# A routed MoE block: the down projection in five products of 128 + 48 features, and router logits with both weight halves side by side

## The chip, the cores and the metric

The kernel runs on one core of one Trainium2 chip. The metric is the device time of one execution in microseconds (us). A core has TensorE (PE; its weight loads are listed as PEld), VectorE (DVE), ScalarE (ACT), GpSimd (POOL) and the queue of SyncE (SP), which issues most of the transfers.

## The reference

A transformer block with adaptive layer norm over 8 batches of 256 tokens of width 256. Attention first, and then a mixture of experts: a router picks two of 8 experts for each token, and a shared expert runs for all. Cut to what matters here:

```python
logits = h @ gate_weight.T                      # 256 -> 8 experts
scores = softmax(logits); topk_w, topk_i = group_limited_topk(scores)   # 2 of 8
g = einsum('th,nfh->ntf', h, gate_w)            # expert: 256 -> 176
u = einsum('th,nfh->ntf', h, up_w)
e = einsum('ntf,nhf->nth', silu(g) * u, down_w) # 176 -> 256
routed = einsum('nth,tn->th', e, wmat)          # weighted sum over the two experts
shared = silu(h @ sh_gate_w.T) * (h @ sh_up_w.T) @ sh_down_w.T
```

## The kernel before

Everything is written by hand: each engine has its own list of steps, in a fixed order, and semaphores tie them together. Products run on operands split in a high part (fp32r) and a low part, the rest. `mm3` (lines 339 to 343) makes one product of two split operands with three instructions: low x high (L341), high x low (L342), high x high (L343).

The first 200 us hold attention for the 8 batches, layer norm, the shared expert (`pe_up`, `pe_down`) and the router, interleaved on all engines. The router of a batch: `pe_logits` multiplies the router weights `wrt` (256 x 8, two blocks of 128 rows, so 2 x `mm3` = six products of 256 columns) with the transposed tokens `h2T` into 8 rows of a bank; `act_lg` copies them to `lg`; for each pair of batches `pe_logits_t` (L551) transposes four pieces of 8 x 128 with the identity, and VectorE selects the experts from the result (`dve_select`). GpSimd scatters each token's row, with its metadata, to the region of its experts in memory (`pool_scatter`).

In the same time the experts' weights are brought in: `sp_weights` (L1254, L1256) loads the gate and up weights and the down weights of one expert into one of two staging buffers `wstage`, `act_weights` (L1271, L1272) copies the high part into `experts_w`, and `split_weights` (L1277, L1278) subtracts it for the low part, on GpSimd or VectorE in turn. The 176 features of the down weights lie as two halves of `FH` = 88 rows side by side.

From some 205 us on the routed loop runs over NT = 39 tiles of 128 rows, as a hardware loop of four tiles a round with a few tiles unrolled at both ends (`steps`). For a tile t, by engine:

- SP loads the 128 rows (`sp_tile`, L1290), after the activation of the tile four earlier.
- TensorE transposes the rows (`pe_tile_in`, L1302, two); `pe_tile_up` makes six products of 352 columns (gate and up); `pe_tile_act` transposes the activation (L1324, two, 88 features each); `pe_tile_down` makes six products of 256 columns, 88 rows each. In one round its order is up(t+1), transposes of the activation(t), transposes of the rows(t+3), down(t-1).
- ScalarE: `act_tile_silu` (L1341) for t+1, the high half of the transposed activation `act_tile_act` (L1345) for t, of the rows `act_tile_in` (L1337) for t+3, and the output copy `act_tile_out` (L1350) for t-1.
- VectorE: metadata (`dve_tile_meta`, L1363 `second`, L1365 `wt`, L1367 `dest`) and activation (`dve_tile_act`, L1374) for t+1, then the low half `dve_tile_lo` (L1380) for t and `dve_tile_in` (L1354) for t+3. The metadata waits until the scatter of the tile four earlier has landed, as `dest` has four buffers.
- GpSimd scatters the 128 output rows (`pool_tile`, L1385) after the copy of L1350.

After the last tile SP reads the routed rows back, and VectorE and GpSimd add them to the residual (`final`).

Of the kernel before, what the change touches and what calls it, by code (L numbers as in the profile page):

```python
# [8 lines left out]
ALU = mybir.AluOpType  # L9
# [7 lines left out]
ds = bass.ds  # L17
# [11 lines left out]
def adaln_block(nc, x_in, w_qkv, b_cols, w_proj, b_proj, gate_col, cam_w0, cam_w1,  # L29
# [12 lines left out]
    FH = F // 2  # L42
    FT = [(f, min(P, FS - f)) for f in range(0, FS, P)]
    UNR = 3
    assert D == KD * P == 256 and S == TT * P == 256 and NT % UNR == 0 and F <= 256

    with ExitStack() as ctx:
# [20 lines left out]
        s_const_dve = sem("const_dve")  # L68
        s_whi_later = sem("whi_later")
        s_wlo_later = sem("wlo_later")  # L70
        s_a_hi = sem("a_hi")
# [166 lines left out]
        wrt = hilo("wrt", [P, KD, NE])  # L238
# [23 lines left out]
        lg = [sb(f"lg{u}", [NE, S]) for u in range(2)]  # L262
# [278 lines left out]
        def act_lg(act, b):  # L541
# [3 lines left out]
            act.activation(lg[b % 2][:], post_bank(b)[0:NE, 0:S], ACT.Copy).then_inc(s_lg_copied, 1)  # L545
# [172 lines left out]
        if True:  # L718
# [80 lines left out]

            def pool_setup(pool):  # L800
# [120 lines left out]
            def dve_guard(dve):  # L921
# [12 lines left out]
                dve.tensor_tensor(mrow[:, 1, :], mrow[:, 0, :], bprow[:], ALU.mult).then_inc(s_mrow_ready, 1)  # L934

# [293 lines left out]
            avT = [tuple(h[0:FH, 1, q * S:(q + 1) * S].rearrange("p (k n) -> p k n", k=2) for h in h2T) for q in range(2)]  # L1229

            sg = [wstage[q][:, 0:F] for q in range(2)]
            av = [wstage[q][:, F:2 * F] for q in range(2)]
            yo = [wstage[q % 2][:, 2 * F + q // 2 * D:2 * F + (q // 2 + 1) * D] for q in range(4)]
# [6 lines left out]
            def expert(e, part, at, n):  # L1240
                base = (0, W1, 2 * W1, 2 * W1 + W2)[part]
                return experts_w[0:(P if part < 2 else FH), ds(e * WE + (base + at), n)]
# [7 lines left out]
            def sp_weights(sp, e, r):  # L1250

                if e >= 2:
# [920 lines left out]
```

## Time and profile before

| | us |
|---|---|
| median of three runs | 331.73 |
| lowest, highest | 330.33, 333.68 |
| profiled execution | 331.29 |
| its span, from the first to the last instruction | 329.5 |
| TensorE busy | 266.7 (81%) |
| VectorE busy | 219.1 (66%) |
| ScalarE busy | 157.2 (48%) |
| GpSimd busy | 147.4 (45%) |

Times in the rows count from the span's start. TensorE's instructions overlap: a product is listed with its whole way through the array (0.28 us for 256 columns), and the next one starts long before its end. What a product costs in a dense stretch is therefore the step from start to start, not the duration. Idle time of an engine is put down to what ended it.

### The profile page before, as it was taken

What the parts mean: (1) busy time and instruction counts of PE and PEld (TensorE: products, weight loads), DVE (VectorE), ACT (ScalarE), POOL (GpSimd) and SP (SyncE); (2) the same over time, 40 slices, a digit from 0 to 9 for tenths busy, and PEclk for the clock granted to TensorE, in tenths of its full rate; (3) what the DMA queues carried; (4) which work ended last, traced back from release to release, by engine and by line L of the source; (5) the groups of instructions that cost most, each with busy time, mean ns of one, the idle gap of its engine ahead of it and who ended that gap; (6) DMA issues with size and microseconds to landing.
All of it is one profiled execution on the core that took longest, in us unless ns stands there. A gap on an engine that the chain in (4) does not pass through costs nothing.

```text
span 329.5 us, 6560 instructions
## 1 busy us (share of the span) xinstructions
PE 266.7 (81%) x1796; PEld 245.4 (75%) x1797; DVE 219.1 (66%) x672; ACT 157.2 (48%) x421; POOL 147.4 (45%) x159
## 2 busy tenths in 40 slices
PE   2799999789999999889968934499999999994000
PEld 2797699579999999779967924499999999993000
DVE  2757664895288735979899984166667766661396
ACT  1457767568466884444423310346555565552000
POOL 2111219612251689568548674014444444444370
PEclk9999999979999999979999996589999999998555
DMA  6990035442012124034201134523434344320894
GB/s 228 315 284 15 1 117 147 130 131 66 32 35 82 50 93 135 0 111 118 50 23 68 58 131 146 178 62 108 125 111 126 115 121 117 111 83 1 289 316 159
DMA packets 30191, 37.78 MB, mean 115 GB/s; under 512 B 4452, under 2 KB 24783, under 8 KB 30168
## 3 DMA queue, kind: packets, MB, share of 16 engines
q1 hardware_dynamic: 25896, 29.02, 29.6%
q0 software_dynamic: 3408, 8.46, 7.3%
q8 instruction: 11, 0.18, 0.2%
q10 hardware_dynamic: 864, 0.02, 0.1%
q14 instruction: 12, 0.10, 0.1%
HBM read 25.83 MB, written 12.57 MB: 117 GB/s over the span
## 4 chain that ended last, share of the span: by engine, by line
PE 61%; DVE 20%; issue 6%; DMA 6%; ACT 3%; SPq 1%; ACTq 1%; POOL 1%; POOLq 0%; DVEq 0%
PE bank L341 14%; PE bank L342 13%; PE bank L343 13%; PE bank L1089 4%; DMA routed_out<-wstage,dest 3%; PE bank L1324 2%; PE bank L1302 2%; PE bank L1072 2%; PE bank L1044 2%; DVE experts_w L1420 2%; DMA experts_w<-routed_out 2%; DVE h2all L499 2%; DVE experts_w L1418 2%; PE bank L1081 1%; DVE aact L440 1%
## 5 line engine op out<-in xcount | busy, mean ns | idle before, releaser
L1385 POOL DMA_INDIRECT routed_out<-wstage,dest x39 | 38.4, 984 | 58.6 <-ACT wstage L1350 40.6
L341 PE MATMUL bank<-experts_w,h2T_lo 128*128 (+1 forms) x156 | 52.8, 338 | 0.6 <-DVE h2T_lo L1354 0.6
L342 PE MATMUL bank<-experts_w,h2T_hi 128*128 (+1 forms) x156 | 48.1, 308 | 0.0
L343 PE MATMUL bank<-experts_w,h2T_hi 128*128 (+1 forms) x156 | 47.9, 307 | 0.0
L662 POOL DMA_INDIRECT routed_in<-h2all,slot_u x32 | 32.6, 1019 | 16.3 <-DVE slot_u L648 8.7
L341 PEld LDWEIGHTS bank<-experts_w,h2T_lo 128*128 128x128 f32 (+1 forms) x156 | 30.2, 194 | 2.4 <-issue 1.7
L342 PEld LDWEIGHTS bank<-experts_w,h2T_hi 128*128 128x128 f32 (+1 forms) x156 | 30.4, 195 | 0.0
L341 PE MATMUL bank<-h2T_hi,wsgu_lo 128*128 128x256 f32 (+1 forms) x96 | 28.3, 294 | 2.3 <-DVE og L458 2.3
L343 PEld LDWEIGHTS bank<-experts_w,h2T_hi 128*128 128x128 f32 (+1 forms) x156 | 30.0, 192 | 0.0
L343 PE MATMUL bank<-h2T_hi,wsgu_hi 128*128 128x256 f32 (+1 forms) x96 | 27.0, 281 | 0.0
L342 PE MATMUL bank<-h2T_lo,wsgu_hi 128*128 128x256 f32 (+1 forms) x96 | 27.0, 281 | 0.0
L1341 ACT ACTIVATE wstage<-bank 128x176 f32<-128x176 f32 x39 | 12.4, 317 | 25.7 <-PE bank L343 25.7
L448 POOL TENSOR_TENSOR aT_lo<-aact,aT_hi 128x256 fp32r<-128x256 f32 (+1 forms) x15 | 11.9, 803 | 24.4 <-ACT aT_hi L431 24.3
L1337 ACT ACTIVATE h2T_hi<-bank 128x256 fp32r<-128x256 f32 x39 | 14.5, 373 | 17.3 <-PE bank L1302 17.1
L341 PE MATMUL bank<-hT_hi,wqk_lo 128*128 128x256 f32 x64 | 20.7, 323 | 1.5 <-DVE hT_lo L1174 1.5
L341 PE MATMUL bank<-wsd_hi,aT_lo 128*128 128x256 f32 (+1 forms) x48 | 14.9, 309 | 7.7 <-DVE aT_lo L448 7.7
L1363 DVE TENSOR_TENSOR second<-exchange,eid_off 128x1 f32<-128x1 f32 x39 | 6.2, 158 | 22.0 <-DMA routed_out<-wstage,dest 22.0
L1350 ACT ACTIVATE wstage<-bank 128x256 f32<-128x256 f32 x39 | 15.0, 384 | 12.2 <-PE bank L343 12.2
L1302 PE MATMUL bank<-ident,exchange 128*128 128x128 f32 x78 | 15.7, 288 | 5.6 <-DMA exchange<-routed_in 5.6
L1354 DVE TENSOR_TENSOR h2T_lo<-bank,h2T_hi 128x256 fp32r<-128x256 f32 x39 | 16.0, 411 | 6.0 <-ACT h2T_hi L1337 6.0
L341 PEld LDWEIGHTS bank<-h2T_hi,wsgu_lo 128*128 128x128 f32 (+1 forms) x96 | 17.4, 181 | 2.6 <-DVE og L458 2.5
L342 PE MATMUL bank<-hT_lo,wqk_hi 128*128 128x256 f32 x64 | 19.3, 301 | 0.0
(225 smaller groups left out, 829.0 us busy)
## 6 DMA issues: line engine op xcount, KB each, us to landing
exchange<-routed_in SPq DMA_DIRECT2D x39, 130.0 KB, 2.1
experts_w<-routed_out SPq DMA_DIRECT2D x16, 256.0 KB, 5.7
wstage<-gu_t SPq DMA_DIRECT2D x8, 352.0 KB
res<-x SPq DMA_DIRECT2D x4, 512.0 KB, 9.2
mx<-modrow SPq DMA_DIRECT2D x8, 256.0 KB, 3.1
mh<-modrow SPq DMA_DIRECT2D x8, 256.0 KB, 3.6
out<-res SPq DMA_DIRECT2D x8, 256.0 KB, 2.3
wmod_s<-w_mod SPq DMA_DIRECT2D x3, 512.0 KB, 10.1
```

Of the source, the lines that this page charges most:

```text
L341: pe.matmul(out_ap, l[1], r[0], start=start, stop=False)
L342: pe.matmul(out_ap, l[0], r[1], start=False, stop=False)
L343: return pe.matmul(out_ap, l[0], r[0], start=False, stop=stop)
L448: eng.tensor_tensor(aT[q % 2][1][0:m, j, :], aact[n % 2][0:m, :], aT[q % 2][0][0:m, j, :].bitcast(F32), ALU.subtract).then_inc(s_a_lo_dve ...
L662: pool.indirect_dma_start(out=routed_in, out_offset=bass.IndirectOffsetOnAxis(slot_u[:, i, j:j + 1], 0), in_=h2all[:, j % (2 * NB), :], in ...
L1089: last = pe.matmul(TR[u][:, t * D:(t + 1) * D], PT[u][:, k, t * P:(t + 1) * P], VV[u][:, k, P:P + D], start=(k == 0), stop=(k == TT - 1))
L1302: last = pe.transpose(XTb[r % 2][:, d * P:(d + 1) * P], xt_in[r][:, d * P:(d + 1) * P], ident[:])
L1337: act.activation(eT[r][0], bank2(XTb[r % 2], P), ACT.Copy).then_inc(s_ex_hi, 1)
L1341: act.activation(sg[r % 2], EGU[r % 2][:, 0:F], ACT.Silu).then_inc(s_esilu, 1)
L1350: act.activation(yo[r], EDN[r % 2][:, 0:D], ACT.Copy).then_inc(s_ey_ready, 1)
L1354: dve.tensor_tensor(eT[r][1], bank2(XTb[r % 2], P), eT[r][0].bitcast(F32), ALU.subtract).then_inc(s_ex_lo, 1)
L1385: pool.indirect_dma_start(out=routed_out, out_offset=bass.IndirectOffsetOnAxis(dest[r][:, 0:1], 0), in_=yo[r], in_offset=None, bounds_chec ...
```

## The change

The activation of a tile is laid out in two blocks of 128 columns for two of 88: features 0 to 127, and then features 128 to 175 twice, at columns 0 to 47 and 64 to 111 of the second block, with zeros between. After the transposes (now 128 columns each) ScalarE writes the high half of all; VectorE writes the low half of the first block, and in the second block it writes the low half over the rows 64 to 111 of the *high* operand. So one operand of 112 rows holds the high and the low half of the 48 features. The down weights are staged the same way, the last 48 rows twice. The down projection then is `mm3` over 128 rows, one product of 112 rows (high and low of the 48 features times the high weights) and one of 48 rows (high times the low weights).

The router's weights stand side by side, 8 high and 8 low columns, so that a product with the high and one with the low half of the tokens give 16 rows; the two sets of 8 are added where they were transposed, by a product with `fold2` (two identities on top of each other, an fp32 product and no longer a transpose). It includes the product of both low parts, which was left out.

Moved or added around it: the down weights of an expert come in three transfers for one; GpSimd sets the rows between to zero before the first one (`pool_stage_rows`), for which SP waits; VectorE makes `fold2` first of all, and the zeros of the activation buffers before the first tile (`dve_tile_gaps`); the activation of a tile has a second multiplication of 48 columns, and the low half is made in two parts.

```diff
-    FH = F // 2
+    FB = F - P
+    HALF = P // 2
...
-        wrt = hilo("wrt", [P, KD, NE])
+        wrt_both = sb("wrt_both", [P, KD, 2 * NE], F32R)
+        wrt = (wrt_both[:, :, 0:NE], wrt_both[:, :, NE:2 * NE])
+        fold2 = sb("fold2", [2 * NE, NE])
...
             for k in range(KD):
-                last = mm3(pe, post_bank(b)[0:NE, 0:S], parts(wrt, slice(None), k),
-                           parts(h2T, slice(None), k, ring4(b)), k == 0, k == KD - 1)
+                for i in range(2):
+                    last = pe.matmul(post_bank(b)[0:2 * NE, 0:S], wrt_both[:, k, :], h2T[i][:, k, ring4(b)],
+                                     start=(k + i == 0), stop=(k + i == KD))
...
-                last = pe.transpose(LOG[:, j * NE:(j + 1) * NE], lg[j // TT][:, j % TT * P:(j % TT + 1) * P], ident[0:NE, 0:NE])
+                last = pe.matmul(LOG[:, j * NE:(j + 1) * NE], lg[j // TT][:, j % TT * P:(j % TT + 1) * P], fold2[:], start=True, stop=True)
...
+            def pool_stage_rows(pool):
+                for r in range(2):
+                    for rows in (slice(P // 4, HALF), slice(HALF + P // 4, P)):
+                        pool.memset(wstage[r][rows, W1 + D:], 0.0).then_inc(s_stage_zero, 1)
+                pool.wait_ge(s_stage_zero, 4)
...
+            def dve_fold2(dve):
+                dve.wait_ge(s_ident_ready, 1)
+                dve.tensor_tensor(fold2[:], ident[0:2 * NE, 0:NE], ident[0:2 * NE, NE:2 * NE], ALU.add)
...
-                sp.dma_start(wstage[r][0:FH, W1:].rearrange("p (j n) -> p j n", j=2),
-                             down_t[ds(e, 1)].rearrange("o (j p) n -> p (o j) n", p=FH)).then_inc((s_est0_in, s_est1_in)[r], 16)
+                down = down_t[ds(e, 1)].rearrange("o f n -> f (o n)")
+                for to, of in ((wstage[r][:, W1:W1 + D], down[0:P]), (wstage[r][0:FB, W1 + D:], down[P:F]),
+                               (wstage[r][HALF:HALF + FB, W1 + D:], down[P:F])):
+                    sp.dma_start(to, of).then_inc((s_est0_in, s_est1_in)[r], 16)
...
-                act.wait_ge((s_est0_in, s_est1_in)[r], 16 * (e - r) + 32)
+                act.wait_ge((s_est0_in, s_est1_in)[r], 64 * (e // 2 + 1))
...
-                    last = pe.transpose(ATb[r % 2][0:FH, j * P:(j + 1) * P], av[r % 2][:, j * FH:(j + 1) * FH], ident[:])
+                    last = pe.transpose(ATb[r % 2][:, j * P:(j + 1) * P], av[r % 2][:, j * P:(j + 1) * P], ident[:])
...
-                for j in range(2):
-                    last = mm3(pe, EDN[r % 2][:, 0:D], parts(avT[r % 2], slice(None), j),
-                               (expert(e, 2, j * D, D), expert(e, 3, j * D, D)), j == 0, j == 1)
-                last.then_inc(s_edn_done, 1)
+                to, (hi, lo) = EDN[r % 2][:, 0:D], avT[r % 2]
+                mm3(pe, to, (hi[:, 0], lo[:, 0]), (expert(e, 2, 0, D), expert(e, 3, 0, D)), True, False)
+                pe.matmul(to, hi[0:HALF + FB, 1], expert(e, 2, D, D, HALF + FB), start=False, stop=False)
+                pe.matmul(to, hi[0:FB, 1], expert(e, 3, D, D, FB), start=False, stop=True).then_inc(s_edn_done, 1)
...
-                dve.scalar_tensor_tensor(av[q], sg[q], wt[q][:, 0:1], EGU[q][:, F:2 * F],
+                dve.scalar_tensor_tensor(av[q][:, 0:F], sg[q], wt[q][:, 0:1], EGU[q][:, F:2 * F], ALU.mult, ALU.mult)
+                dve.scalar_tensor_tensor(av[q][:, P + HALF:F + HALF], sg[q][:, P:F], wt[q][:, 0:1], EGU[q][:, F + P:2 * F],
                                          ALU.mult, ALU.mult).then_inc(s_ea_ready, 1)
...
-                dve.tensor_tensor(avT[q][1], bank2(ATb[q], P)[0:FH], avT[q][0].bitcast(F32), ALU.subtract).then_inc(s_ea_lo, 1)
+                hi, lo = avT[q]
+                second_copy = slice(HALF, HALF + FB)
+                dve.tensor_tensor(lo[:, 0], ATb[q][:, 0:P], hi[:, 0].bitcast(F32), ALU.subtract)
+                dve.tensor_tensor(hi[second_copy, 1], ATb[q][second_copy, P:2 * P], hi[second_copy, 1].bitcast(F32),
+                                  ALU.subtract).then_inc(s_ea_lo, 1)
+
+            def dve_tile_gaps(dve):
+                dve.wait_ge(s_split_pool, NE // 2)
+                for q in range(2):
+                    dve.memset(av[q][:, P:2 * P].rearrange("p (i n) -> p i n", i=2)[:, :, FB:HALF], 0.0)
...
+                    sp.wait_ge(s_stage_zero, 4)
                     sp_weights(sp, 0, 0)
```

## Rows read from the trace of the kernel before

**Rows 1.** Table by stretches: stretch, busy PE, PEld, DVE, ACT, POOL (instructions), clock, DMA share, GB/s.
```profile
230.47:284.87 54.40, 54.40 (x401) 52.33 (x400) 37.55 (x151) 31.57 (x101) 24.58 (x25) 1.00 0.40 118
```

**Rows 2.** Timeline, TensorE in one tile of the loop: start, us, engine, line, operation, shapes.
```profile
242.38 0.37 PE L341 MATMUL bank<-experts_w,h2T_lo 88*128 x1
...
243.07 0.28 PE L343 MATMUL bank<-experts_w,h2T_hi 88*128 x1
243.07 0.19 PEld L341 LDWEIGHTS bank<-experts_w,h2T_lo 128*128 128x128 f32 x1
243.19 0.32 PE L341 MATMUL bank<-experts_w,h2T_lo 128*128 x1
...
244.50 0.37 PE L341 MATMUL bank<-experts_w,h2T_lo 88*128 x1
```

**Rows 3.** Timeline, the circle through scatter, metadata, activation, down products and copy.
```profile
242.30 0.98 POOL L1385 DMA_INDIRECT routed_out<-wstage,dest  x1 [1.14 <-ACT wstage L1350]
...
242.82 0.16 DVE L1363 TENSOR_TENSOR second<-exchange,eid_off 128x1 f32<-128x1 f32 x1 [0.57 <-DMA routed_out<-wstage,dest]
...
243.33 0.40 DVE L1374 SCALAR_TENSOR_TENSOR wstage<-wstage,wt,bank 128x176 f32<-128x176 f32 x1
...
243.65 0.41 DVE L1380 TENSOR_TENSOR h2T_lo<-bank,h2T_hi 88x256 fp32r<-88x256 f32 x1
...
243.99 0.28 PEld L1324 LDWEIGHTS bank<-ident,wstage 128*88 128x88 f32 x2
...
244.91 0.16 DVE L1363 TENSOR_TENSOR second<-exchange,eid_off 128x1 f32<-128x1 f32 x1 [0.52 <-DMA routed_out<-wstage,dest]
...
245.51 0.38 ACT L1350 ACTIVATE wstage<-bank 128x256 f32<-128x256 f32 x1 [0.29 <-PE bank L343]
...
246.73 0.98 POOL L1385 DMA_INDIRECT routed_out<-wstage,dest  x1 [1.14 <-ACT wstage L1350]
```

**Rows 4.** The chain that ended last, at the loop's head: start, us, what.
```profile
223.93 0.41 DVE wstage L1374
224.39 0.42 PE bank L1324 x2
```

**Rows 5.** Timeline, TensorE around one set of the logits' transposes.
```profile
158.79 0.28 PE L343 MATMUL bank<-h2T_hi,wsgu_hi 128*128 128x256 f32 x1
159.00 0.32 PEld L551 LDWEIGHTS bank<-ident,lg 8*128 8x128 f32 x4
...
159.34 0.38 PE L341 MATMUL bank<-h2T_hi,wsgu_lo 128*128 128x256 f32 x1
...
159.56 0.28 PE L342 MATMUL bank<-h2T_lo,wsgu_hi 128*128 128x256 f32 x1
```

**Rows 6.** Timeline, TensorE from the rank products into the next ones.
```profile
185.28 0.24 PE L568 MATMUL bank<-r_both,ones 128*128 128x8 bf16 x4
185.38 0.36 PE L341 MATMUL bank<-h2T_hi,wsgu_lo 128*128 128x256 f32 x1
```

**Rows 7.** Timeline, TensorE from the last logits product into the next ones.
```profile
78.34 0.28 PE L343 MATMUL bank<-h2T_hi,wrt_hi 128*8 128x256 f32 x1
78.46 0.59 PE L1089 MATMUL bank<-VV,exchange 128*128 128x256 f32 x2
```

**Rows 8.** Groups by shape, 230 to 280 us: busy us, mean ns, idle before.
```profile
L1367 DVE SCALAR_TENSOR_TENSOR dest<-second,exchange 128x1 uint32<-128x1 f32 x24 | 3.7, 152 | 0.0
```

**Rows 9.** Timeline and chain near the start: the modulation's products, one product of 256 columns.
```profile
6.39 3.56 PE L954 MATMUL bank<-cS,wmod_s 128*128 128x8 f32 x16 [6.39 <-DVE cS L865]
...
15.37 0.21 PE bank L343
```

**Rows 10.** Timeline of SP and ScalarE: the last expert's down weights and who waits.
```profile
151.63 0.42 SPq L1256 DMA_DIRECT2D wstage<-down_t  x1
...
156.05 0.79 ACT L1271 ACTIVATE experts_w<-wstage 128x704 fp32r<-128x704 f32 x1 [1.30 <-DMA wstage<-down_t]
```

**Rows 11.** Table by stretches, columns as in rows 1.
```profile
160.00:180.00 20.00, 15.77 (x135) 14.68 (x134) 19.11 (x57) 5.68 (x16) 10.99 (x13) 1.00 0.10 34
```

More of the change, by code:

```diff
@@ L41, in adaln_block @@
     ROW = D + META
-    FH = F // 2
+    FB = F - P
+    HALF = P // 2
     FT = [(f, min(P, FS - f)) for f in range(0, FS, P)]
     UNR = 3
-    assert D == KD * P == 256 and S == TT * P == 256 and NT % UNR == 0 and F <= 256
+    assert D == KD * P == 256 and S == TT * P == 256 and NT % UNR == 0 and 0 < FB <= 48
     with ExitStack() as ctx:
@@ L67, in adaln_block @@
         s_x3p_in = sem("x3p_in")
-        s_const_dve = sem("const_dve")
         s_whi_later = sem("whi_later")
         s_wlo_later = sem("wlo_later")
+        s_stage_zero = sem("stage_zero")
         s_a_hi = sem("a_hi")
@@ L259, in adaln_block @@
         slot_u = sb("slot_u", [P, 2, NR], U32)
-        lg = [sb(f"lg{u}", [NE, S]) for u in range(2)]
+        lg = [sb(f"lg{u}", [2 * NE, S]) for u in range(2)]
         sact = [sb(f"sact{u}", [P, S]) for u in range(2)]
@@ L544, in act_lg @@
                 act.wait_ge(s_lt_done, b // 2)
-            act.activation(lg[b % 2][:], post_bank(b)[0:NE, 0:S], ACT.Copy).then_inc(s_lg_copied, 1)
+            act.activation(lg[b % 2][:], post_bank(b)[0:2 * NE, 0:S], ACT.Copy).then_inc(s_lg_copied, 1)
         def pe_logits_t(pe, p):
@@ L1228, in adaln_block @@
             eT = [tuple(h[:, 0, q * S:(q + 1) * S].rearrange("p (k n) -> p k n", k=KD) for h in h2T) for q in range(4)]
-            avT = [tuple(h[0:FH, 1, q * S:(q + 1) * S].rearrange("p (k n) -> p k n", k=2) for h in h2T) for q in range(2)]
+            avT = [tuple(h[:, 1, q * S:(q + 1) * S].rearrange("p (k n) -> p k n", k=2) for h in h2T) for q in range(2)]
             sg = [wstage[q][:, 0:F] for q in range(2)]
-            av = [wstage[q][:, F:2 * F] for q in range(2)]
-            yo = [wstage[q % 2][:, 2 * F + q // 2 * D:2 * F + (q // 2 + 1) * D] for q in range(4)]
+            av = [wstage[q][:, F:F + 2 * P] for q in range(2)]
+            yo = [wstage[q % 2][:, F + 2 * P + q // 2 * D:F + 2 * P + (q // 2 + 1) * D] for q in range(4)]
             second = [tb(f"second{r}", [P, 1]) for r in range(2)]
@@ L1238, in adaln_block, with expert @@
             pad = exchange[:, 4 * ROW:5 * ROW]
-            def expert(e, part, at, n):
+            def expert(e, part, at, n, rows=P):
                 base = (0, W1, 2 * W1, 2 * W1 + W2)[part]
-                return experts_w[0:(P if part < 2 else FH), ds(e * WE + (base + at), n)]
+                return experts_w[0:rows, ds(e * WE + (base + at), n)]
             def bank2(t, n=256):
@@ L1271, in act_weights @@
                 act.activation(expert(e, 0, 0, W1), wstage[r][:, 0:W1], ACT.Copy)
-                act.activation(expert(e, 2, 0, W2), wstage[r][0:FH, W1:], ACT.Copy).then_inc(s_ew_hi, 1)
+                act.activation(expert(e, 2, 0, W2), wstage[r][:, W1:], ACT.Copy).then_inc(s_ew_hi, 1)
             def split_weights(eng, e):
@@ L1277, in split_weights @@
                 eng.tensor_tensor(expert(e, 1, 0, W1), wstage[r][:, 0:W1], expert(e, 0, 0, W1).bitcast(F32), ALU.subtract)
-                eng.tensor_tensor(expert(e, 3, 0, W2), wstage[r][0:FH, W1:], expert(e, 2, 0, W2).bitcast(F32),
+                eng.tensor_tensor(expert(e, 3, 0, W2), wstage[r][:, W1:], expert(e, 2, 0, W2).bitcast(F32),
                                   ALU.subtract).then_inc((s_split_pool, s_split_dve)[r], 1)
@@ L1344, in act_tile_act @@
                 act.wait_ge(s_eat_done, t + 1)
-                act.activation(avT[r % 2][0], bank2(ATb[r % 2], P)[0:FH], ACT.Copy).then_inc(s_ea_hi, 1)
+                act.activation(avT[r % 2][0], bank2(ATb[r % 2], P), ACT.Copy).then_inc(s_ea_hi, 1)
             def act_tile_out(act, t, r):
@@ L1496, in _ @@
                     pool_setup(pool)
+                    pool_stage_rows(pool)
                     pool_rstd1(pool, 0, 1)
@@ L1782, in _ @@
                 def _(dve):
+                    dve_fold2(dve)
                     dve_silu(dve)
@@ L1949, in one @@
                             dve_tile_in(dve, t + 3, (r + 3) % 4)
+                    dve_tile_gaps(dve)
                     for t in range(2):
```

## The prediction

> **What bounds the kernel now.** I read the table by stretches first, then the page, then the timelines of one tile. In the routed loop TensorE never rests: between 230.47 and 284.87 us it is busy for the whole 54.40 us at a granted clock of 1.00, while VectorE is busy for 37.55, ScalarE for 31.57 and GpSimd for 24.58 us with 25 scatters [rows 1]. That is 54.40 / 25 = 2.176 us for each tile. A busy TensorE is not yet TensorE at its limit, so I looked at the starts: a tile's first product of the down projection starts at 242.38 and the next tile's at 244.50, 2.12 us apart (some 0.06 us more on average, the jump of the loop of four tiles). From the last of the six to the first of the up projection is 243.07 to 243.19, so 0.12 us is what one product of 256 columns costs [rows 2].
>
> There is a second circle, nearly as long. A tile's scatter must land before VectorE may compute the metadata of the tile four later, and the activation of that tile, the transposes, the down projection, the copy and the next scatter hang behind it. Read in the timeline: metadata 242.82, activation 243.33, its end 243.73, transpose weights 243.99, first down product 244.50, copy 245.51, scatter 246.73; from a scatter's start to the next metadata it is 242.30 to 244.91, 2.61 us [rows 3]. Sum: 0.51 + 0.40 + 0.26 + 0.51 + 1.01 + 1.22 + 2.61 = 6.52 us, and this serves three tiles (the down products behind tile t+1's transposes are tile t's). Only the 0.26 between activation and transposes holds slack: where TensorE really waited for the activation it followed 0.05 us after its end (223.93 + 0.41 to 224.39) [rows 4]. So the circle needs 6.52 - 0.21 = 6.31 us for three tiles, 2.10 a tile, against TensorE's 2.176. Whatever relieves TensorE by more than 0.07 us a tile meets this circle.
>
> **The routed down projection.** Six products of 88 rows become three of 128 rows, one of 112 and one of 48. One product less is 0.12 us. The number of rows by itself costs nothing that the trace shows: products of 88 rows start 0.12 apart, and one of 128 rows follows one of 88 without a gap [rows 2].
>
> But 48 rows may be another thing. Outside this change the kernel has one operation with few rows, the transposes of the logits (8 rows), sixteen times, always in the same rhythm. The product before them starts at 158.79, and their weight load starts only at 159.00, although weight loads otherwise start with the product before (243.07 and 243.07 in [rows 2]). The product after them is listed at 159.34, and the one behind it at 159.56, 0.22 later instead of 0.12 [rows 5]. Is this due to the few columns that are streamed? No: the rank products of 8 columns but 128 rows flow into the next ones at 185.28 and 185.38 [rows 6]. Is it due to a small output? No: the router's products, 8 output rows but 128 operand rows, have the usual 0.12 step on leaving (78.34 to 78.46) [rows 7]. What is left is the number of operand rows: going from many rows to few and back empties the array, and the next weights are not loaded ahead.
>
> I price that for a 48-row product of 256 columns. Entering: the load waits until 0.21 us after the start of the product before (158.79 to 159.00), and the product then streams 0.10 behind its load (0.22 - 0.12): 0.31 instead of 0.12, so 0.19 us more. Leaving costs the same again, since the up product behind it must wait for a 256-column product in the same way: 0.19. Together 0.38 us, against 0.12 saved: TensorE needs 2.176 - 0.12 + 0.38 = 2.44 us a tile, 0.26 more. Bounds: if the empty array costs only the shifts in the list (0.09 in, 0.11 out), it is 0.20 - 0.12 = 0.08 more; if each way costs 0.04 more than I read (the list rounds to 0.01, and the first of the four transposes follows its load by a further 0.02), 0.46 - 0.12, some 0.33 more; if 48 rows do not count as few, nothing is added. 48 lies between 8, where it happens, and 88, where it does not; which side it is on is the main question of this forecast. I take the side of 8, because 48, like 8, leaves more than half of the 128 rows unused, and 88 does not. The Trainium skill, page TensorEngine Tiling (Array Packing), sections Key Properties and When to Use Tiling, says it outright: "Changing tiling mode (not just tile) drains the TensorE", and a contraction of up to 64 is a row-tiled one. The rule gives no number; by it the sum is the one with 0.38, and the trace agrees for 8 rows; no run here shows it for 48.
>
> **The other parts of a tile.** VectorE gets a second multiplication of 128x48. The nearest prices: 152 ns for 128x1 and 398 (in the loop 0.40 us) for 128x176 of the same kind [rows 3, 8]; by columns 0.15 + 47 x 0.0014 = 0.22 us. The first one hands over after 0.32 us (243.33 to 243.65), so the activation is ready at 0.32 + 0.22 instead of 0.40: 0.14 later; I take 0.15, with the bounds 0.07 and 0.32 (as dear as the big one). The low half splits in two of the same total width; its end comes 0.15 plus about 0.1 for a second start, at 244.3 instead of 244.06, still ahead of the products at 244.50, which must follow the transposes. ScalarE's copy and the transposes change only from 88 to 128 partitions or weight columns. Without the emptied array the circle would be 6.31 + 0.15 - 0.12 = 6.34, 2.11 a tile. With it, 0.19 of entering is added, 6.53, 2.18 a tile: below TensorE's 2.44. So TensorE stays the bound, and VectorE's new work is hidden behind it.
>
> **Sum of the routed part.** Thirty tiles in the steady part at 0.26: 7.8 us. At the head the chain goes from the first landing to the activation (223.93) [rows 4]: the first tile's down and one activation lie in it, 0.19 - 0.12 + 0.15 = 0.2. At the tail, where no more rows are transposed, the chain is again that of landings; two rounds and the last tile's low half count there: 2 x 0.22 + 0.1 = 0.5. Together 8.5 us.
>
> **The router.** Sixteen products less (two for each of eight batches) are 16 x 0.12 = 1.9 us of TensorE. The fold is dearer than the transposes it replaces: the only full-precision product with 8 columns, that of the modulation, goes as two instructions each, 16 in 3.56 us at the start of the kernel, 0.22 each [rows 9]. That stretch runs at half the speed of later ones (a 256-column product takes 0.21 us at 15 us, 0.12 later) [rows 2, 9], so 0.11 at full speed is the upper bound; from below, the four transposes' loads take 0.32 for four [rows 5], some 0.06 each behind the first. Eight for four are then 0.25 to 0.54 us more for each of four pairs, 1.0 to 2.2 in all; I take 1.4 (the rows are few, as in the lower row). Net -0.5 us, and as VectorE, busy for 19.11 of the 20 us from 160 on [rows 11], sets the pace of the last pairs, I count -0.3 (bounds -0.9 to +0.3). The 16-row fold is as much a product of few rows as the 8-row transpose: no new emptying.
>
> **Loads and start.** Each expert's down weights go in three transfers for one: two more issues of 0.42 us on the queue of SP [rows 10]. For the last expert ScalarE already waits 1.30 us for that landing (156.05) [rows 10], so it may start 0.9 us later; behind it stand a gate and the copy of logits, which had about a microsecond to spare. I take +0.2, bounds 0 and 0.9. The four small memsets on GpSimd, the fold matrix and the two gap memsets on VectorE lie where these engines wait for loads (before 5 us) or for the first tile (200 to 209 us): nothing, at most 0.3 us if a cover is gone.
>
> **Total.** Profiled execution before 331.3 us (span 329.5 and 1.8 around it), median of the runs 331.7. 331.3 + 8.5 - 0.3 + 0.2 = 339.7, so 340.
>
> **Rivals.** (A) *The forecast:* 48 rows empty the array. Own range by the bounds of that price, 0.08 to 0.33 a tile: 334.5 to 342.5 us. (B) *48 rows are like 88.* Then TensorE needs 2.06 a tile, less than the circle of the scatter, 2.11, which binds: 30 x (2.176 - 2.11) = 2.0 saved, -0.3 and +0.2 elsewhere: 329.3 us (331.5 if the second multiplication costs 0.32). For it speaks that 88 and 96 rows show nothing. The skill, page TensorE: Matmul & The Clock Gate, section Why this matters for your kernels, has a product of 32 rows take the same time as one of 128; alone it would mean this case, but the 8-row rhythm in the trace contradicts it as soon as the two kinds alternate. (C) *Faster, the whole saving kept:* the array is not emptied and the circle is shorter than I read, 6.17 us for three tiles or less, for which the scatter must take 0.17 us less from start to metadata than 2.61, or the second multiplication must cost nothing. Then 30 x 0.12 = 3.6 less: 327.7 us. Against it: the slack of 0.21 is small and the second multiplication must take some time. (D) *The weights come late and nothing else happens:* B plus 0.9 and the dear fold: about 331.
>
> **Chances.** A 0.62; B and D together 0.30; C 0.08. A change of 1% (3.3 us) is about what a measurement of this kernel can tell from none. Slower by more than that: A without its lowest end, 0.60. Within: B, D and that end, 0.31. Faster: C and a bit of B, 0.09. The range 329.0 to 341.5 takes in B, D and all but the top of A; A's own range stands above.
>
> **What would show it.** Right: a loop period near 2.4 us; in a tile's list, the weight load of the 48-row product about 0.21 us behind the start of the product before, and the first up product's load as late again; VectorE's wait for the scatter's landing shorter than its present 0.5 us or gone. Wrong (B): all five products 0.12 apart, period 2.11, TensorE idle before the transposes with VectorE's activation as releaser. Wrong in size: the period tells it, 2.25 or 2.5. For the router: steps of 0.06 or 0.11 between the fold's eight instructions. For the loads: ScalarE's wait near 156 us grown from 1.3 to 2.2.

## The result, and the profile after

| | before | after |
|---|---|---|
| median of the runs, us | 332.71 (4 runs, 330.33 to 335.89) | 338.50 (4 runs, 336.68 to 340.26) |
| ratio, with its 95% interval | | 1.022 (1.0165 to 1.0275) |
| profiled execution, us | 331.29 | 338.31 |
| its span, us | 329.5 | 336.5 |
| TensorE: busy us, instructions | 266.7, 1796 | 274.0, 1757 |
| VectorE: busy us, instructions | 219.1, 672 | 236.2, 753 |

The changed kernel is slower by 2.2%. The ratio leaves out executions in a slower state of the kernel before, so it isn't the ratio of the two medians. 39 TensorE instructions less are listed, and they keep TensorE busy for 7.3 us more. The routed loop has the table by stretches as its first witness (columns as in [rows 1]; the stretch goes from the end of one output copy to that of the copy 25 tiles later, as there):

```profile
230.59:290.52 59.93, 59.93 (x377) 52.66 (x376) 48.31 (x201) 31.54 (x100) 24.60 (x25) 1.00 0.36 107
```

That is 59.93 / 25 = 2.397 us a tile, where [rows 1] has 2.176. TensorE is still busy without a break, at the same granted clock of 1.00, and with fewer instructions (377 for 401). VectorE has risen from 37.55 us to 48.31, which is 1.93 a tile: near its limit, but not at it.

The kernel by its pieces, from the two traces (ends of the output copies, L1350 before and L1366 after):

| stretch | before | after | difference |
|---|---|---|---|
| start to the first tile's load | 205.40 | 204.61 | -0.8 |
| to the copy of the first tile | 14.12 | 14.00 | -0.1 |
| to the fifth tile's | 8.84 | 9.58 | +0.7 |
| to the 35th tile's | 65.51 | 71.91 | +6.4 |
| to the last tile's | 7.10 | 7.35 | +0.25 |
| to the end | 28.49 | 29.02 | +0.5 |

Nine tenths of the loss lie in the thirty steady tiles. One tile there, in TensorE's timeline of after (products and weight loads mixed; L344 to L346 are `mm3`, L1348 is the product over 112 rows, L1349 the one over 48):

```profile
251.08 0.28 PE L346 MATMUL bank<-experts_w,h2T_hi 128*128 x1
251.09 0.19 PEld L1348 LDWEIGHTS bank<-experts_w,h2T_hi 112*128 112x128 f32 x1
...
251.20 0.28 PE L1348 MATMUL bank<-experts_w,h2T_hi 112*128 x1
...
251.41 0.18 PEld L1349 LDWEIGHTS bank<-experts_w,h2T_hi 48*128 48x128 f32 x1
251.41 0.38 PE L1349 MATMUL bank<-experts_w,h2T_hi 48*128 x1
...
251.72 0.19 PEld L344 LDWEIGHTS bank<-experts_w,h2T_lo 128*128 128x128 f32 x1
251.72 0.43 PE L344 MATMUL bank<-experts_w,h2T_lo 128*128 x1
...
251.99 0.32 PE L345 MATMUL bank<-experts_w,h2T_hi 128*128 x1
```

The load of the 112-row product starts with the product before it (251.09 and 251.08). The load of the 48-row product doesn't: it comes 0.21 us after the start of the product before (251.20 to 251.41). The load behind it comes 0.31 later still, and the second up product 0.27 after the first, where the steps inside the up projection are 0.16. From the start of the 112-row product to the second up product it is 0.79 us; with the usual steps it would be 0.12 + 0.12 + 0.16 = 0.40. So entering and leaving 48 rows costs 0.39 us a tile, for a product of 0.12 that was saved.

VectorE's metadata still waits for the landing of an earlier scatter, but for 0.38 us here where it was 0.57 and 0.52 in [rows 3]; the circle over the scatter has slack:

```profile
250.87 0.16 DVE L1379 TENSOR_TENSOR second<-exchange,eid_off 128x1 f32<-128x1 f32 x1 [0.38 <-DMA routed_out<-wstage,dest]
```

Where the activation was one multiplication, there are now two: it ends 1.09 us after the metadata's start, where it was 0.92.

### The profile page after: what moved, and what is told of

It is laid out like the page before. It is cut to its first block, busy times and chain, and to the rows that moved or that the text cites. A ratio compares the mean times of both kernels' runs of the same rounds, so it can differ in the third digit from the quotient of the medians.

```text
span 336.5 us, 6583 instructions
## 1 busy us (share of the span) xinstructions
PE 274.0 (81%) x1757; PEld 245.9 (73%) x1758; DVE 236.2 (70%) x753; ACT 157.0 (47%) x421; POOL 148.7 (44%) x163
## 4 chain that ended last, share of the span: by engine, by line
PE 64%; DVE 20%; issue 6%; DMA 4%; ACT 2%; SPq 1%; ACTq 1%; POOL 1%; POOLq 0%; DVEq 0%
PE bank L344 15%; PE bank L346 12%; PE bank L345 12%; PE bank L1349 3%; PE bank L1103 3%; PE bank L1318 3%; PE bank L1340 2%; PE bank L1058 2%; PE bank L1086 2%; DMA experts_w<-routed_out 2%; DVE experts_w L1444 2%; DVE experts_w L1446 2%; DVE h2all L502 2%; DMA exchange<-routed_in 1%; PE bank L1095 1%
## 5 line engine op out<-in xcount | busy, mean ns | idle before, releaser
L344 PE MATMUL bank<-experts_w,h2T_lo 128*128 x117 | 44.4, 379 | 0.8 <-DVE h2T_lo L1370 0.6
L346 PE MATMUL bank<-experts_w,h2T_hi 128*128 x117 | 37.0, 316 | 0.0
L345 PE MATMUL bank<-experts_w,h2T_hi 128*128 x117 | 36.9, 315 | 0.0
L344 PE MATMUL bank<-h2T_hi,wsgu_lo 128*128 128x256 f32 (+1 forms) x96 | 28.9, 301 | 2.0 <-DVE og L461 2.0
L346 PE MATMUL bank<-h2T_hi,wsgu_hi 128*128 128x256 f32 (+1 forms) x96 | 27.7, 288 | 0.0
L344 PEld LDWEIGHTS bank<-experts_w,h2T_lo 128*128 128x128 f32 x117 | 22.5, 193 | 6.2 <-issue 1.6
L345 PEld LDWEIGHTS bank<-experts_w,h2T_hi 128*128 128x128 f32 x117 | 22.7, 194 | 0.0
L344 PE MATMUL bank<-hT_hi,wqk_lo 128*128 128x256 f32 x64 | 20.7, 323 | 2.4 <-DVE hT_lo L1188 2.4
L346 PEld LDWEIGHTS bank<-experts_w,h2T_hi 128*128 128x128 f32 x117 | 22.5, 192 | 0.0
L1366 ACT ACTIVATE wstage<-bank 128x256 f32<-128x256 f32 x39 | 15.0, 384 | 14.7 <-PE bank L1349 14.7
L344 PE MATMUL bank<-wsd_hi,aT_lo 128*128 128x256 f32 (+1 forms) x48 | 14.8, 307 | 6.2 <-DVE aT_lo L451 6.2
L344 PEld LDWEIGHTS bank<-h2T_hi,wsgu_lo 128*128 128x128 f32 (+1 forms) x96 | 18.1, 188 | 2.3 <-DVE og L461 2.2
L346 PE MATMUL bank<-hT_hi,wqk_hi 128*128 128x256 f32 x64 | 19.2, 300 | 0.0
```

Of the source, the lines that this page charges most:

```text
L344: pe.matmul(out_ap, l[1], r[0], start=start, stop=False)
L345: pe.matmul(out_ap, l[0], r[1], start=False, stop=False)
L346: return pe.matmul(out_ap, l[0], r[0], start=False, stop=stop)
L1366: act.activation(yo[r], EDN[r % 2][:, 0:D], ACT.Copy).then_inc(s_ey_ready, 1)
```

## The experiments

All ratios are against the kernel before, run on the same chip beside the version, with 95% intervals; a time without a ratio is one execution. The median of before differs with the chip: 333.6 us beside the first four versions under after, 331.0 beside after without the circle and the last two of the table, 330.5 beside the other four. A period is the time a tile takes between the ends of the copies of tiles 5 and 30, counted from 0, in one profiled execution. The three values of 2.41 to 2.42 hold one long tile of 2.83 to 2.94 us at the start of the loop; their other tiles take 2.38 to 2.41, as in after.

| version | ratio or one time | period |
|---|---|---|
| before | | 2.176 |
| after | 1.022 (1.017 to 1.028) | 2.397 |
| 48-row product over 112 rows | 1.010 (1.006 to 1.014) | 2.258 |
| over 72 rows | 336.9 us | 2.261 |
| over 64 rows | 340.7 us | 2.416 |
| two products of 48 rows in a row | 343.0 us | 2.414 |
| routed part alone | 1.021 (1.017 to 1.024) | 2.415 |
| router alone | 1.002 (0.998 to 1.005) | 2.187 |
| before, without the scatter's circle | 0.990 (0.988 to 0.993) | 2.122 |
| after, without the scatter's circle | 1.025 (1.019 to 1.030) | 2.394 |
| 112 rows, without the circle | 0.981 (0.978 to 0.983) | 2.014 |
| the same, router of before | 0.981 (0.978 to 0.984) | 2.018 |
| 112 rows, no second multiplication | 329.9 us | 2.196 |

### Is it the number of rows?

The low weights of the 48 features lie twice in the staging too, and the rows between are zero. So the fifth product can run over more rows than it needs. Over 112 rows it also adds the product of both low parts, and nothing else changes.

```diff
-                pe.matmul(to, hi[0:FB, 1], expert(e, 3, D, D, FB), start=False, stop=True).then_inc(s_edn_done, 1)
+                pe.matmul(to, hi[0:HALF + FB, 1], expert(e, 3, D, D, HALF + FB), start=False, stop=True).then_inc(s_edn_done, 1)
```

> The changed kernel, but the fifth down product runs over 112 rows for 48 (it adds low part x low part of the 48 features, nothing is left out). Theory (few rows empty the array): the five products start 0.12 us apart, TensorE needs 2.06 us a tile, and the circle through the scatter, 6.31 + 0.17 - 0.12 = 6.36 us for three tiles, sets a period of 2.12 us; the time is 338.5 - 30 x (2.40 - 2.12) = about 330 us. Rival 1 (something else about the new fifth product costs, e.g. that VectorE writes into the high operand): period stays 2.40, time 338. Rival 2 (no such circle): period 2.06, about 328.

Measured: 337.27 us, ratio 1.0102 (1.0064 to 1.014), period 2.258. TensorE's timeline, one tile:

```profile
255.38 0.28 PE L346 MATMUL bank<-experts_w,h2T_hi 128*128 x1
255.50 0.28 PE L1348 MATMUL bank<-experts_w,h2T_hi 112*128 x1
255.62 0.28 PE L1349 MATMUL bank<-experts_w,h2T_hi 112*128 x1
255.74 0.32 PE L344 MATMUL bank<-experts_w,h2T_lo 128*128 x1
255.89 0.32 PE L345 MATMUL bank<-experts_w,h2T_hi 128*128 x1
```

Every step is 0.12, and the up product follows as closely. A product with 64 more rows, none of which the result needs, takes away the whole 0.39 us in TensorE's list. That the rows are the cause is shown. But the period fell by 0.14 only, not by 0.39: something else took over. That part of the expectation failed; it is followed up below.

The same edit with 64 and with 72 rows looks for the border:

> The changed kernel with 64 rows in the fifth product for 48 (16 of them zeros). Theory (what counts is whether the rows are more than half of 128): same as the changed kernel, the weight load 0.21 us behind the product before, period 2.40. Rival (each number of rows below 88 costs in proportion to what is missing): smaller delays than with 48 rows, period about 2.3.

> The changed kernel with 72 rows in the fifth product for 48. Theory (the border is at half of the rows): no delay at all, steps of 0.12, period 2.12 as with 112 rows. Rival (in proportion): a delay near that of 64 rows, period 2.3 to 2.4.

Measured: 340.65 us with a period of 2.416 for 64 rows, 336.94 us with 2.261 for 72 (not the 2.12 expected, for the same reason as with 112). The timeline of 64 rows:

```profile
251.41 0.28 PE L1348 MATMUL bank<-experts_w,h2T_hi 112*128 x1
251.62 0.38 PE L1349 MATMUL bank<-experts_w,h2T_hi 64*128 x1
251.93 0.43 PE L344 MATMUL bank<-experts_w,h2T_lo 128*128 x1
252.20 0.32 PE L345 MATMUL bank<-experts_w,h2T_hi 128*128 x1
```

The steps are 0.21, 0.31, 0.27, as with 48 rows; with 72 rows they are 0.13, 0.12, 0.17. The price doesn't grow with the rows: it is there or not, and the border lies between 64 and 72. The Trainium skill, page TensorEngine Tiling (Array Packing), section Key Properties, says that changing the tiling mode drains TensorE, and its section When to Use Tiling counts a contraction of up to 64 rows as one for row tiling. The lateness in these two runs agrees with both, and the page has no number for the drain, the runs do. That a tiling mode is what changes here no run shows: the code asks for none, and the timelines show only when TensorE is late.

### Is it paid for each product or at each crossing?

The product with the high weights also over 48 rows; its low part of the activation is left out of the sum. Two products of few rows then follow each other.

```diff
-                pe.matmul(to, hi[0:HALF + FB, 1], expert(e, 2, D, D, HALF + FB), start=False, stop=False)
+                pe.matmul(to, hi[0:FB, 1], expert(e, 2, D, D, FB), start=False, stop=False)
```

> The changed kernel with the fourth down product over the 48 high rows alone (left out: the low part of the 48 features times the high weights), so two 48-row products stand side by side. Theory (entering and leaving cost, not the product): still 2.40 us a tile, the second 48-row product 0.12 behind the first. Rival (each 48-row product costs by itself): 0.2 to 0.4 us more, a period of 2.6 to 2.8.

Measured: 342.98 us, period 2.414. The timeline:

```profile
251.61 0.28 PE L346 MATMUL bank<-experts_w,h2T_hi 128*128 x1
251.82 0.38 PE L1348 MATMUL bank<-experts_w,h2T_hi 48*128 x1
252.04 0.28 PE L1349 MATMUL bank<-experts_w,h2T_hi 48*128 x1
252.25 0.43 PE L344 MATMUL bank<-experts_w,h2T_lo 128*128 x1
252.52 0.32 PE L345 MATMUL bank<-experts_w,h2T_hi 128*128 x1
```

The one step of entering has moved forward (251.61 to 251.82); the second product of 48 rows is listed 0.22 behind the first and not the 0.12 expected, and the next one only 0.21 behind it instead of 0.31. The sum tells: from L346 to the second up product it is 0.91 us, the same as in the changed kernel (251.08 to 251.99). The period is the same within 0.02. The expected 0.2 to 0.4 us more for a price of each product isn't there. So the price belongs to the crossings, not to the products: one visit with two products costs what one with one product costs.

### Which of the two edits carries the loss?

The changed kernel with the router code of before, and the kernel before with the router edit alone (the lines of the diff that speak of `wrt_both`, `fold2` and `lg`).

> The changed kernel's routed down with the router of before. Theory (the routed down carries all of the loss, the router edit nothing): 0.5 to 1.5 us of the loss is not the router's, so a ratio of 1.018 to 1.024 against before, the same as with both edits, and a period of 2.40 us in the routed stage. Rival (the router edit saves what its six fewer wide products are worth, about 2 us, in both): then this version is slower than both together by some 1.5 to 2 us, a ratio of 1.027. Rival (the eight folding products a pair, at 0.111 us each and 0.2 at their entering and leaving, cost more than is saved): a ratio of 1.018 or less.

> The kernel before with the router edit alone: logits in four products for six, and small folding products in place of transposes. Theory: within 1 us of the kernel before (saved 4 pairs x 0.48 = 1.9 us on the logits, given back 4 x about 0.6 = 2.4 us on the folding where it isn't covered), ratio 0.997 to 1.004; the period of the routed stage unchanged at 2.18. Rival: the saving stands, ratio 0.994. The two single edits' differences should add up to that of both, within 1 us.

Measured: 1.0206 (1.0173 to 1.0238), and 1.0015 (0.9982 to 1.0049). The routed part carries the loss, and the two differences add up to that of both, 2.2%. The interval of the first leaves out the 1.027 of one rival, but not the upper end of the other, 1.018. The router edit is worth nothing that can be measured: the rival with the saving left standing, 0.994, lies outside its interval, while a cost of up to 0.5% does not. A sum of rows accounts for it. One folding of a pair of batches, from the timelines of TensorE and its weight loads after (L555 is the folding product):

```profile
100.22 0.28 PE L346 MATMUL bank<-wsd_hi,aT_hi 96*128 96x256 f32 x1
100.43 1.05 PE L555 MATMUL bank<-fold,lg 16*128 16x8 f32 x8
101.41 0.44 PE L1086 MATMUL bank<-ident,exchange 128*128 128x128 f32 x2
...
100.43 0.96 PEld L555 LDWEIGHTS bank<-fold,lg 16*128 16x128 f32 x8
```

The weight loads of eight folding instructions take 0.96 us, where those of the four transposes took 0.32 [rows 5]. For four pairs that is 2.6 us more, against 16 x 0.12 = 1.9 us less for the logits. The crossing is there before and after alike (0.21 from 100.22 to 100.43).

### What took over at 2.258?

In the version with 112 rows TensorE waits once in most rounds of four tiles for the activation, and then has two gaps. In its timeline (weight loads and VectorE stand behind the products):

```profile
252.02 0.44 PE L1340 MATMUL bank<-ident,wstage 128*128 128x128 f32 x2
252.30 0.38 PE L1318 MATMUL bank<-ident,exchange 128*128 128x128 f32 x2
252.63 0.38 PE L344 MATMUL bank<-experts_w,h2T_lo 128*128 x1
...
253.21 0.28 PE L1349 MATMUL bank<-experts_w,h2T_hi 112*128 x1
253.64 0.42 PE L344 MATMUL bank<-experts_w,h2T_lo 128*128 x1
...
252.02 0.20 PEld L1340 LDWEIGHTS bank<-ident,wstage 128*128 128x128 f32 x2 [0.19 <-DVE wstage L1391]
...
251.71 0.26 DVE L1391 SCALAR_TENSOR_TENSOR wstage<-wstage,wt,bank 128x48 f32<-128x48 f32 x1
...
252.18 0.29 DVE L1400 TENSOR_TENSOR h2T_hi<-bank,h2T_hi 48x128 fp32r<-48x128 f32 x1
```

The transposes' load at 252.02 starts 0.05 us after the end of the second multiplication (251.71 + 0.26). Behind it the steps are 0.33 from 252.30 where 0.14 is usual, and 0.43 from 253.21 where 0.12 is usual; the second gap stands at the end of a round. The first gap is a wait too. The down products need the low half, and its second part ends at 252.18 + 0.29 = 252.47, 0.16 before the product at 252.63. From 240 us on no down product of this version starts closer behind the low half than 0.16, and in all nine tiles where the step from the transposes of the rows is over 0.14, 0.16 to 0.34, it is just 0.16. In the kernel before, where the low half is one instruction, it is 0.16 as well where TensorE had waited (224.66 to 224.82), and the step is only 0.18 (224.64 to 224.82). So the split low half makes TensorE some 0.15 us later than a whole one would, each time it waits for the activation. The same place in the kernel before:

```profile
224.25 0.41 DVE L1380 TENSOR_TENSOR h2T_lo<-bank,h2T_hi 88x256 fp32r<-88x256 f32 x1
...
224.38 0.16 PEld L1324 LDWEIGHTS bank<-ident,wstage 128*88 128x88 f32 x2 [0.36 <-DVE wstage L1374]
...
224.64 0.38 PE L1302 MATMUL bank<-ident,exchange 128*128 128x128 f32 x2
...
224.82 0.38 PE L341 MATMUL bank<-experts_w,h2T_lo 88*128 x1
```

VectorE hardly rests either: in its timeline of this version the metadata of two tiles starts at 253.01 and 255.11, and all between goes back to back. Two candidates, then: the circle over the scatter, or VectorE's own work. The next version tells them apart by taking the scatter out of the circle. Each tile gets its own column of `dest`, so VectorE need not wait for the scatter of four tiles earlier; ScalarE waits for that one instead, one step later in its list, before it writes the same output buffer.

```diff
-            dest = [tb(f"dest{r}", [P, 1], U32) for r in range(4)]
+            dest = tb("dest", [P, NT], U32)
...
-                if not (type(t) is int and t < 4):
-                    dve.wait_ge(out_sems[r], 4 * (t - r))
...
-                dve.scalar_tensor_tensor(dest[r][:], second[q][:], float(T), xt_in[r][:, D + 3:D + 4],
+                dve.scalar_tensor_tensor(dest[:, ds(t, 1)], second[q][:], float(T), xt_in[r][:, D + 3:D + 4],
...
+                        if back and not (type(t) is int and t < 4):
+                            act.wait_ge(out_sems[r], 4 * (t - r))
                         if back:
                             act_tile_out(act, t - 1, (r - 1) % 4)
```

> The fifth product over 112 rows (no emptying of the array), and the circle over the scatter taken out: each tile has its own column of scatter indices, VectorE doesn't wait for the scatter of four tiles earlier, and ScalarE waits for it instead before it writes the same output buffer again, 2 us later in the round. If the circle over the scatter held the period at 2.26: it falls to between 2.06 and 2.12, TensorE's own sum, and the time by 30 x 0.15 to 0.2 = 4.5 to 6 us, to about 331 beside 333.6 of before (ratio 0.992). If VectorE's own work holds it (2.06 us of instructions from the first of the metadata to the end of the tile's split, back to back, and another 0.05 to 0.2 in the round's jump): 2.15 to 2.25, a ratio of 1.002 to 1.009, and its instructions stay back to back.

> The kernel before with the circle over the scatter taken out in the same way. In the prediction TensorE sets its period of 2.18 and the circle has 2.10 a tile: then nothing changes, or at most the round's jump of 0.06 a tile goes (30 x 0.06 = 1.8 us, ratio 0.995). If the circle held the kernel before, the ratio is under 0.99.

Measured: 324.1 us, ratio 0.9806 (0.9777 to 0.9834), period 2.014 for the version with 112 rows; 327.11 us, ratio 0.9904 (0.9878 to 0.993), period 2.122 for the kernel before. Both gained more than was expected. The version with 112 rows went below the 2.06 to 2.12 named for TensorE's sum, as that sum still held the 0.06 of the jump; VectorE's own work, named at 2.15 to 2.25, doesn't hold it there. The circle held the version with 112 rows at 2.258. It also had a part in the kernel before: 2.176 - 2.122 = 0.054 us a tile, which the prediction read as the jump of the loop. That is 1.6 us of the 3.4 by which the medians differ; in the two profiled executions the steady tiles gain 1.9 us, the first four 0.3 and those behind the 35th 0.6. TensorE at the same place of a round, in the version with 112 rows and no circle:

```profile
246.37 0.29 PE L1348 MATMUL bank<-experts_w,h2T_hi 112*128 x1
246.50 0.28 PE L1349 MATMUL bank<-experts_w,h2T_hi 112*128 x1
246.62 0.33 PE L344 MATMUL bank<-experts_w,h2T_lo 128*128 x1
```

No gap: 0.12. In the other rounds of this version the jump costs about 0.1 at most. The large gaps at the end of a round, 0.39 to 0.53 us, come only in tiles where TensorE has just had to wait. That its own list then runs too late to hide the jump is my reading of it; it is argued, not shown.

What is left there is a loop in which two engines are full. TensorE: 2.12 - 0.12 = 2.00 us. VectorE, from its timeline without the circle:

```profile
247.77 0.15 DVE L1376 TENSOR_TENSOR second<-exchange,eid_off 128x1 f32<-128x1 f32 x1
...
248.64 0.26 DVE L1388 SCALAR_TENSOR_TENSOR wstage<-wstage,wt,bank 128x48 f32<-128x48 f32 x1
248.81 0.28 DVE L1396 TENSOR_TENSOR h2T_lo<-bank,h2T_hi 128x128 fp32r<-128x128 f32 x1
249.11 0.29 DVE L1397 TENSOR_TENSOR h2T_hi<-bank,h2T_hi 48x128 fp32r<-48x128 f32 x1
249.44 0.42 DVE L1370 TENSOR_TENSOR h2T_lo<-bank,h2T_hi 128x256 fp32r<-128x256 f32 x1
249.78 0.15 DVE L1376 TENSOR_TENSOR second<-exchange,eid_off 128x1 f32<-128x1 f32 x1
```

From metadata to metadata 2.01 us without a wait. The low half takes 249.44 - 248.81 = 0.63, where it took 0.33 in one instruction (243.65 to 243.98 before).

The changed kernel itself, without the circle, shows whether the circle had a part in its loss:

> The changed kernel with nothing but the circle over the scatter taken out. The theory (TensorE with the emptied array sets its 2.40 us; the circle has slack there) says: period 2.39 to 2.42 and the time unchanged within 2 us of the changed kernel, a ratio of 1.015 to 1.022. If the circle had a part in the loss, the period falls towards 2.25 and the ratio to about 1.005.

Measured: 338.2 us, ratio 1.0245 (1.0193 to 1.0298), period 2.394 for 2.397. It had none. The two versions without the circle also give the purest price of the crossings: 2.394 - 2.014 = 0.38 us a tile, for 48 rows against 112 with all else alike.

What the second multiplication does in a loop that the circle binds:

```diff
-                dve.scalar_tensor_tensor(av[q][:, P + HALF:F + HALF], sg[q][:, P:F], wt[q][:, 0:1], EGU[q][:, F + P:2 * F],
-                                         ALU.mult, ALU.mult).then_inc(s_ea_ready, 1)
```

> The version with 112 rows and the circle in place, without VectorE's second multiplication: the operand's lower copy is zero there, so the weights' low half of the 48 features and the low half of the activations are left out of the sum. It asks what the second multiplication costs in a loop that the circle binds. It lies 0.17 us in the path from scatter to scatter: over three tiles a turn 0.06, over four 0.04 a tile, so 2.20 to 2.22 for 2.258. If the gap of 0.43 us that TensorE shows once in four tiles goes as well because the activation comes earlier: 2.12 to 2.16. If VectorE's own work held the period: 2.09.

Measured: 329.93 us, period 2.196. The period falls by 0.062. The gap stays (0.44 us once a round), and so does the step of 0.32 to 0.34 before the down products, which still wait for the split low half. Whether the 0.17 us are shared by three tiles, 0.057, or by four, 0.043, the two executions don't tell: over 24 tiles, six whole rounds, the difference is 0.03 to 0.06 by the tile at which one begins. VectorE's own 2.10 - 0.17 isn't reached.

### The best version

The last one takes what the others showed: the routed part with both 48-feature products over 112 rows, no circle over the scatter, and the router of before.

> The best combination the readings so far point to: fifth product over 112 rows, the circle over the scatter taken out, and the router of before. If the router edit is worth nothing (its own run: 1.0015), this is the same as the version with the new router, a ratio of 0.978 to 0.984 and a period of 2.01; if the four transposes a pair for eight folding products matter where TensorE is waited for, 0.5 us less.

Measured: 324.32 us, ratio 0.9809 (0.9776 to 0.9842), period 2.018. The same as with the new router (324.1 us, 0.9806). Against the changed kernel it is 0.981 / 1.022, 4% faster. Its gain has two parts that only work together: the changed kernel with 112 rows loses 1.0%, taking out the circle alone gives 1.0%, both give 1.9%. So once the circle is gone, the five products in place of six are worth 0.9% (324.1 beside 327.11 us, the router edit included).

## Why the prediction came out as it did

**The emptied array: right, in kind and size.** The likeliest case said 48 rows side with 8 and cost 0.38 us a tile. The list of after shows 0.39, and the pair without the circle 0.38. The sign it named is there word for word: the load 0.21 us late [rows 5], on the way in. On the way out it is 0.31 in the list, not "as late again", since the 48-row product is listed with its load; only the sum of both ways was right. The border, left open between 8 and 88, lies between 64 and 72, so the reason given ("leaves more than half of the 128 rows unused") holds too.

**The period: 2.40 and not 2.44.** The step that was off is the base. The prediction added to 2.176, "some 0.06 us more on average, the jump of the loop". This 0.06 was no fixed cost of TensorE. It came from the waits on the circle, and with TensorE slower the circle had slack: 2.12 - 0.12 + 0.39 = 2.39. The run of before without the circle has 2.122. Thirty tiles at the measured steady 0.22 make 6.6 (the table has 6.4), not 7.8.

**Head and tail.** 0.2 and 0.5 were counted. The first four tiles after the first copy took 0.7 more and the stretch from the 35th copy on 0.75, while the way from the first load to the first copy took 0.1 less. The head was mis-sized because it counted one tile, where four already run at the new period. Together with the steady tiles the routed part cost 7.8 us for 8.5. That the total came so near is in part luck: the steady tiles were counted 1.4 us too dear, head and tail 0.65 too cheap.

**VectorE's second multiplication: right.** 0.14 to 0.15 was counted, 0.17 measured, and TensorE hid it. **The split low half: mis-sized.** "About 0.1 for a second start" was 0.30: the two take 0.63 for 0.33. An instruction over 48x128 takes 0.30 us where 128x128 takes 0.28, so the fewer rows save nothing here. It didn't count in the changed kernel, with 1.93 us of VectorE under 2.40. In the version with 112 rows it did, as the first gap shows: "still ahead of the products" fails there. In the best version VectorE has no pause, but without the circle TensorE finds the activation ready about 0.5 us early; whether the low half costs time there no run shows.

**The router: a gain of 0.3 was counted, none is there.** The folding was taken near the lower row, "1.4", because its rows are few; it is 0.64 a pair, 2.6 us, and so above the upper bound of 2.2. The step between its instructions is 0.11, as that bound had it. From the first load to the next product it is 0.98 us (100.43 to 101.41), of which eight such steps are 0.89: the bound left out the remaining 0.1, the step on leaving. The router's own run gives 1.0015 (0.998 to 1.005), which holds -0.3 us as well as +1: the size isn't settled by times, only by the rows.

**The loads: right in place, smaller.** ScalarE's wait for the last expert's down weights grew, but to 1.65 us and not to 2.2, and most of the growth is ScalarE being free earlier against the load. From the first issue of the down weights to ScalarE's start it is 4.48 us (150.82 to 155.30) where it was 4.42 (151.63 to 156.05) [rows 10]: the two more transfers cost 0.06 and not up to 0.9. I see nothing later that moved by it: the first tile's load came 0.8 us earlier than before, which is within what two executions differ by (the first copy ends at 216.9 us in one of the profiled executions and at 223.6 in another). Timelines of ScalarE and SP after:

```profile
155.30 0.79 ACT L1287 ACTIVATE experts_w<-wstage 128x704 fp32r<-128x704 f32 x1 [1.65 <-DMA wstage<-down_t]
...
150.82 1.95 SPq L1273 DMA_DIRECT2D wstage<-down_t  x3
```

**The rival B would have been wrong by itself.** It said that products of enough rows give a period of 2.11 and 329.3 us. The version with 112 rows is that case, and has 2.258 and a ratio of 1.010. Its circle of three tiles is as long as worked out where TensorE comes to it late: scatter 250.41, metadata 253.01, end of the activation 254.10, and from the transposes' load (254.59) to the copy (255.93) and the scatter (257.15) 2.56, with the 0.05 between them 6.30 us, 2.10 a tile. Two things were left out. The first is the low half. Where TensorE waits for the activation, the down products then wait for the low half, and from the transposes' load to the copy it is 1.51 us (252.02 to 253.53) instead of 1.34: 6.47, 2.16 a tile. The second is the gap at the end of the round that follows. The way scatter 248.32, metadata 250.88, transposes 252.02, copy 255.93, scatter 257.15 takes 8.83 us for four tiles, 2.21. It holds one turn of TensorE, from 252.02 to the next transposes' load at 254.59, and this turn takes 2.57 us with its gaps instead of 2.01. The period of 2.258 makes 9.03 for four tiles, but the first four tiles take 9.33; the five rounds behind them take 8.84 to 9.00, 8.94 on average, and what holds them 0.1 above 8.83 stays open. The rival C needed a circle 0.17 us shorter; the circle read here is longer, not shorter.

## What to carry to other kernels

Before you pack a rest of features into a product of fewer rows, compare it with the same product padded with zeros to more than half of the rows (72 were enough, 64 were not): here the padded one has the same step of 0.12 us, and the short one costs 0.39 us at its crossings. If short products can't be avoided, put them next to each other, as one visit costs the same with one product as with two. And when an engine that sets the period is relieved, look first for the circle right below it, and count each way through it, here the low half beside the activation; then break it (here with one more column of indices a tile) in the same step, or the saving doesn't arrive.

## What the hardware showed that I had not expected

- 48 and 64 rows cost the same, 72 and 112 rows nothing (2.416 and 2.261 us a tile for 64 and 72); the numbers of rows between 64 and 72 were not tried.
- The round's jump costs TensorE about 0.1 us at most when it needn't wait (2.014 us a tile), and some 0.3 us behind a real wait (253.21 to 253.64). The other late start of that tile (252.30 to 252.63) is a second wait, for the low half: 0.16 us after its end, every time.
- On VectorE 48x128 takes 295 ns and 128x128 283 ns on average in the loop of the changed kernel; the rows saved are worth nothing.
- A full-precision product of 16 rows into 8 columns goes as two instructions, with a step of 0.11 us for each, while a transpose of the same piece took one instruction, four of them with loads of 0.32 us in all.
